# Layer 1's query product in two row tiles of 64 into two banks, with the product of keys and values packed

## The chip, the core and the metric

The kernel runs on one core of a Trainium2 chip. The core has five engines that work side by side and meet at semaphores: TensorE (matmuls, PE in the profile; PEld is its loading of weights), VectorE (DVE), ScalarE (ACT), GpSimd (POOL) and SyncE (SP), which issues the DMA transfers here. TensorE writes only to PSUM, eight banks of 128 partitions x 512 floats; VectorE and ScalarE read them. TensorE's clock has two levels, 1.2 and 2.4 GHz. The metric is the device time of one execution in microseconds.

## The reference, cut to what matters

Two conditioned attention layers over x of 32 sequences x 128 tokens x 512. Layer 0 is ordinary attention with 16 heads. Layer 1 is linear attention with 8 heads of 64, and the change is in it:

```python
xn = _ln(x, ln_w, ln_b)
q = xn @ Wq + bq
k = xn @ Wk + bk + (1.0 - src_mask) * -1000000.0
q = jax.nn.softmax(q.reshape(b, t, h, dh), axis=-1)   # h = 8, dh = 64
k = jax.nn.softmax(k.reshape(b, t, h, dh), axis=1)
v = ((xn @ Wv + bv) * src_mask).reshape(b, t, h, dh)
att = jnp.einsum('bnhd,bnhl->bhdl', k, v)
y = jnp.einsum('bnhd,bhdl->bnhl', q, att).reshape(b, t, d)
...
hh = _ln(y, ln2_w, ln2_b) * (1.0 + scale) + shift
hh = jax.nn.silu(hh) @ W_out + b_out
return x + hh
```

`att` is one 64 x 64 matrix for each head, and `y` multiplies each token's 64 query features of a head with it.

## The kernel before, in words

The sequences are worked in pairs (GROUP = 2), 16 pairs for each layer. One step of the program holds the attention and output of a pair k, the projections (keys, values, queries) of the next pair f, and the norm of the pair n after it. Steps 16 to 31 work layer 1's pairs (`step1` on each engine); most of them run in a loop whose body holds two steps. The order on each engine is written out by hand in `step1`, and engines meet at counting semaphores; nothing schedules it anew. Projections are exact-split float products: a matmul is written as three passes (lines 1276 to 1278).

The path around the change, for sequence b (0 or 1) of pair k:
- ScalarE's `k_exps` (line 644) takes the exponentials of a pair's keys, behind VectorE's maxima (`k_soft`, line 966).
- TensorE turns keys and queries (`turn_k` line 1387, `turn_q` line 1395) and ScalarE copies them out of PSUM (`kt_out` line 656, `qt_out` line 661). Both sequences' turned queries go to bank 3, one behind the other. In ScalarE's step the order is: copies of keys 0, queries 0 and keys 1; `k_out` and `k_exps` of pair f, first half; the copy of queries 1; `k_out` and `k_exps`, second half.
- `keys_values` (line 1407): for each of the four chunks c of 128 features, two matmuls of 64 x 64, one for each head, in two column tiles. They land on the diagonal blocks of a 128 x 128 square in bank 4.
- `kv_out` (line 1008) scales them on VectorE with two instructions, one for each diagonal half, into `kv_blocks`, whose off-diagonal blocks GpSimd has set to zero once, in the last step of layer 0 (the wait for `zeroed` is VectorE's).
- `query` (line 1417): for each chunk one matmul of 128 x 128 with the block-diagonal square, so two heads at once, into bank 5 (b = 0) or 1 (b = 1).
- `y_norm` (line 932) multiplies by the reciprocal of the softmax's sum, then come statistics (line 880), GpSimd's norm (lines 454 to 462), TensorE's turn (`turn_yn`, line 1368), the film scale (line 941), GpSimd's addition of the shift (line 488), tanh (line 632), silu (line 948), and the output product and its addition to x (line 960). SyncE stores x (line 331) and then loads the next x (line 316).

`claim(bank, ...)` makes TensorE wait for whoever last had to read the bank before it writes there again.

TensorE's step reads: turn k0, q0, k1; output of the last pair's second sequence; keys 0; turn q1; `keys_values` 0; keys 1; `query` 0; `keys_values` 1; values 0; `query` 1; queries 0; turn y0; values 1; turn y1; queries 1; turn x0; output 0; turn x1.

Of the kernel before, what the change touches and what calls it, by code (L numbers as in the profile page):

```python
# [8 lines left out]
ALU = mybir.AluOpType  # L9
# [3 lines left out]
P = 128  # L13
GROUP = 2
# [27 lines left out]
def done(stage, at):  # L42

    if at.reg is None and at.const < stage.first:
        return stage.always
    return stage.sem, (at + (1 - stage.first)).value()
# [9 lines left out]
def build(nc, t, out):  # L56
    B, T, D = t["x"].shape
    TE = t["cond_2048"].shape[1]
    C = D // P
    KE = TE // P  # L60
    N = GROUP * P
    G = B // GROUP
# [13 lines left out]
    H0, H1 = layers[0]["H"], layers[1]["H"]  # L76
# [7 lines left out]
    with ExitStack() as ctx:  # L84
# [3 lines left out]
        def sem(name):  # L88
            return ctx.enter_context(nc.semaphore(name))

        def chunks(ap):
            return ap.rearrange("p (c n) -> p c n", c=C)
# [76 lines left out]

        bank = [ctx.enter_context(nc.psum_tensor(f"bank{i}", [P, D], F32)) for i in range(8)]  # L170
        FIRST = dict(X=(0, 1), PT=(4, 5), Q=(6, 7), K=(0, 1), V=(3, 4), PV=(7, 7), Y=(2, 2), H=(6, 7), O=(5, 6))
        SECOND = dict(X=(0, 1), K=(6, 7), V=(0, 6), Q=(2, 4), KT=(2, 4), QT=(3, 3), KV=(4, 4), Y=(5, 1), H=(3, 7), O=(5, 7))

        MIXED = FIRST | dict(K=(6, 7), V=(0, 1), Q=(3, 4))

# [4 lines left out]
        per_seq = prob[:].rearrange("p a h n -> p (a h n)").rearrange("p (j d) -> p j d", d=D)  # L180
        k_tok = [per_seq[:, b, :] for b in range(GROUP)]
        q_feat = [per_seq[:, GROUP + b, :] for b in range(GROUP)]
        kv_blocks = [per_seq[:, 2 * GROUP + b, :] for b in range(GROUP)]
        k_max = sb("k_max", [P, 2, 2 * GROUP])
        k_sum = sb("k_sum", [P, 2, 2, 2 * GROUP])
        k_rec = sb("k_rec", [P, 2, 2, 2 * GROUP])
# [23 lines left out]
        w_in = [[sem(f"w_in{l}{j}") for j in range(4)] for l in range(2)]  # L210
        w_high = [[sem(f"w_high{l}{j}") for j in range(4)] for l in range(2)]
        w_split = [[sem(f"w_split{l}{j}") for j in range(4)] for l in range(2)]
        zeroed = sem("zeroed")
        wide_clear = sem("wide_clear")

        def stages(names, first=0):
# [218 lines left out]
        def _(pool):  # L435
# [70 lines left out]
            def step0(i, n, f, k, late, slot):  # L506
                norm1(n, 0)
                if i == 0:
                    pool.wait_ge(par_in[0], PARS[0])
                residual(0, k, 0)  # L510
                norm1(n, 1)
                norm2(k, 0)
                residual(0, k, 1)
                v_mask(f, slot, 0)
                if i == 0:
                    pool.wait_ge(film_dve, 3)
                add_shift(0, k, 0)
                norm2(k, 1)
                v_mask(f, slot, 1)
                if i == G - 1:  # L520

                    for g in range(2):
                        pool.wait_ge(*done(s[f"pt_pe{g}"], LAST0))
                    pool.memset(per_seq[:, 2 * GROUP:3 * GROUP, :], 0.0).then_inc(zeroed, 1)
                add_shift(0, k, 1)

            def step1(i, n, f, k, late, slot):
# [277 lines left out]
        def _(dve):  # L805
# [35 lines left out]
            def bias_col(l, j, i, b):  # L841
                dve.wait_ge(par_in[l], PARS[l])
                dve.wait_ge(bias_sum_pe, TURN[l, j])
                dve.tensor_tensor(col[:, l, i, :], col[:, l, i, :], bank[b][:, 0:C], ALU.add).then_inc(bias_dve, 1)
# [76 lines left out]
            def y_norm(l, k, kslot, b):  # L921
                dve.wait_ge(*done(s["y_pe"], k + b))
                dve.wait_ge(*done(s["stats2"], k + (b - 1)))
                dve.wait_ge(*done(s["yn_full"], k + (b - 1)))
                if l == 0:
                    dve.wait_ge(*done(s["rec"], k + b))
                    yb, h, rc = bank[FIRST["Y"][b]], H0, rec0[:, b, :]
                else:
                    dve.wait_ge(*done(s["qrec"], k + b))
                    yb, h, rc = bank[SECOND["Y"][b]], H1, q_rec[:, kslot, b, :]  # L930
                hv = lambda ap: ap.rearrange("p (h e) -> p h e", h=h)
                dve.tensor_tensor(hv(y_s[:]), hv(yb[:]),
                                  rc.rearrange("p (h o) -> p h o", o=1).broadcast_to([P, h, D // h]),
                                  ALU.mult).then_inc(s["y_norm"].sem, 1)
                dve.wait_ge(*done(s["y_norm"], k + b))
                moments(1, b, y_s[:], "stats2", "aggr2", k + b)

# [63 lines left out]
            def kv_out(k, kslot, b):  # L1001
                dve.wait_ge(*done(s["pv"], k + b))
                dve.wait_ge(*done(s["y_pe"], k + (b - GROUP)))
                dve.wait_ge(*done(s["krec"], k))
                for h in range(2):
                    q2 = slice(DH1 * h, DH1 * (h + 1))
                    rc = k_rec[q2, kslot].rearrange("p a (j g) -> p (a j) g", g=GROUP)[:, :, b:b + 1]
                    last = dve.tensor_tensor(chunks(kv_blocks[b])[q2, :, q2], chunks(bank[SECOND["KV"][b]][:])[q2, :, q2],
                                             rc.broadcast_to([DH1, C, DH1]), ALU.mult)
                last.then_inc(s["att_out"].sem, 1)  # L1010

            def start():
                f = pair(0)
# [32 lines left out]
            def step0(i, n, f, k, late, slot):  # L1046
                if late:
                    film_scale(0, late + (-1), 1)
                if i == G - 3:
                    spread_norm_b(1)  # L1050
                softmax(k, 0, (0, 1))
                if i == 0:
                    film(0, 5)
                if late:
                    silu(late + (-1), 1)
                softmax(k, 0, (2,))
                if late:
                    s_low_part(late + (-1), 1)
                softmax(k, 0, (3,))
                stats1(n, 0)  # L1060
                softmax(k, 1, (0, 1, 2))
                if late:
                    output(FIRST, late + (-1), 1)
                if i == 0:
                    embed_sum(1, 0, 6)
                softmax(k, 1, (3,))
                stats1(n, 1)
                sums_inverse(k, 0)
                y_norm(0, k, 1 - slot, 0)
                sums_inverse(k, 1)  # L1070
                v_add(0, FIRST, f, slot, 0)
                if i == 0:
                    embed_sum(1, 1, 6)
                if i == G - 3:
                    bias_col(1, WK, KB, 6)
                    dve.wait_ge(mask_saved, 16)
                    dve.wait_ge(film_dve, 3)
                film_scale(0, k, 0)
                if i == G - 2:
                    low_part(1, WK, (0, 1))  # L1080
                silu(k, 0)
                if i == G - 2:
                    bias_wide(1, WV, VALUE_BIAS[1], 3)
                y_norm(0, k, 1 - slot, 1)
                s_low_part(k, 0)
                xt_low(n, 1 - slot, 0)
                xt_low(n, 1 - slot, 1)
                v_add(0, FIRST, f, slot, 1)
                if i == G - 2:
                    low_part(1, WK, (2, 3))  # L1090
                    low_part(1, WV)
                output(FIRST, k, 0)
                if i == 0:
                    film(1, 6)
# [37 lines left out]
            def step1(i, n, f, k, late, slot):  # L1132
                if i == G:
                    film_scale(0, late + (-1), 1)
                    q_sums(k, 1 - slot, 0)
                    silu(late + (-1), 1)
                    q_sums(k, 1 - slot, 1)
                    s_low_part(late + (-1), 1)
                    dve.wait_ge(zeroed, 1)
                elif late:  # L1140
                    output(SECOND, late + (-1), 1)
                if n:
# [60 lines left out]
        def _(pe):  # L1203
# [194 lines left out]
            def keys_values(k, kslot, b):  # L1398
                to = SECOND["KV"][b]
                claim(to, (s["att_out"], k + b))  # L1400
                pe.wait_ge(*done(s["kt_out"], k + b))
                pe.wait_ge(*done(s["v_mask"], k + b))
                for c in range(C):
                    for h in range(2):
                        rows = slice(DH1 * h, DH1 * (h + 1))
                        head = slice(c * P + DH1 * h, c * P + DH1 * (h + 1))
                        last = pe.matmul(bank[to][rows, head], k_tok[b][:, head], v_s[:, kslot, b, head],  # L1407
                                         start=True, stop=True, tile_position=(0, DH1 * h))
                last.then_inc(s["pv"].sem, 1)

            def query(k, b):
                to = SECOND["Y"][b]
                claim(to, (s["y_norm"], k + b))
                pe.wait_ge(*done(s["att_out"], k + b))
                pe.wait_ge(*done(s["qt_out"], k + b))
                for c in range(C):
                    last = pe.matmul(bank[to][:, c * P:(c + 1) * P], q_feat[b][:, c * P:(c + 1) * P],  # L1417
                                     kv_blocks[b][:, c * P:(c + 1) * P], start=True, stop=True)
                last.then_inc(s["y_pe"].sem, 1)

            def start():
# [178 lines left out]
```

## Time and profile before

| | us |
|---|---|
| median of 3 runs (1095.82 to 1096.64) | 1095.91 |
| the profiled execution | 1097.78 |
| its span | 1096.0 |
| TensorE busy | 1054.8 (96%) |
| VectorE busy | 759.8 (69%) |
| ScalarE busy | 591.6 (54%) |
| GpSimd busy | 448.6 (41%) |

The span is what the trace covers; the execution's time has 1.78 us beside it. Busy times are sums over instructions. A float matmul is recorded as two passes, so the 128 matmuls of the query product stand in the trace as 256. Passes overlap: a pass lasts longer than the distance from its start to the next one's, and it is this distance that counts in a stream. "Idle before" is the time in which an engine had nothing to do ahead of an instruction, with the one that ended it.

### The profile page before, as it was taken

What the parts mean: (1) busy time and instruction counts of PE and PEld (TensorE: products, weight loads), DVE (VectorE), ACT (ScalarE), POOL (GpSimd) and SP (SyncE); (2) the same over time, 40 slices, a digit from 0 to 9 for tenths busy, and PEclk for the clock granted to TensorE, in tenths of its full rate; (3) what the DMA queues carried; (4) which work ended last, traced back from release to release, by engine and by line L of the source; (5) the groups of instructions that cost most, each with busy time, mean ns of one, the idle gap of its engine ahead of it and who ended that gap; (6) DMA issues with size and microseconds to landing.
All of it is one profiled execution on the core that took longest, in us unless ns stands there. A gap on an engine that the chain in (4) does not pass through costs nothing. (4 is left out here: it accounts for less than half of the span.)

```text
span 1096.0 us, 25953 instructions
## 1 busy us (share of the span) xinstructions
PE 1054.8 (96%) x8696; PEld 909.8 (83%) x8696; DVE 759.8 (69%) x1326; ACT 591.6 (54%) x1960; POOL 448.6 (41%) x783
## 2 busy tenths in 40 slices
PE   6999999999999999999999999999999999999995
PEld 4878888888888888888887778888888888888884
DVE  4656766676666766667678787777777777777764
ACT  5366667776677766776588443433343443434431
POOL 3242434334343343433343344444444444444432
PEclk9999999999999999999999999999999999999997
DMA  8824110111101111011102211111111111111011
GB/s 275 256 84 141 42 61 24 62 62 41 60 24 62 62 41 59 25 62 63 43 23 98 95 50 33 40 55 57 57 57 57 57 57 57 52 52 39 31 38 58
DMA packets 46017, 71.65 MB, mean 65 GB/s; under 512 B 10256, under 2 KB 14448, under 8 KB 45968
## 3 DMA queue, kind: packets, MB, share of 16 engines
q1 hardware_dynamic: 45968, 71.02, 20.3%
q8 instruction: 27, 0.44, 0.2%
q14 instruction: 22, 0.18, 0.1%
HBM read 54.19 MB, written 16.79 MB: 65 GB/s over the span
## 5 line engine op out<-in xcount | busy, mean ns | idle before, releaser
L1276 PE MATMUL bank<-xt_hi,w_hi 128*128 128x256 f32 x768 | 228.4, 297 | 3.1 <-DVE xt_lo L893 3.1
L1277 PE MATMUL bank<-xt_lo,w_hi 128*128 128x256 f32 x768 | 218.5, 284 | 0.0
L1278 PE MATMUL bank<-xt_hi,w_lo 128*128 128x256 f32 x768 | 218.3, 284 | 0.0
L454 POOL TENSOR_SCALAR stat<-stat 128x1 f32<-128x1 f32 x128 | 34.5, 270 | 441.8 <-DVE stat L884 417.7
L613 ACT ACTIVATE prob<-prob,neg_max 128x128 f32<-128x128 f32 x512 | 198.7, 396 | 6.7 <-DVE neg_max L907 6.6
L632 ACT ACTIVATE th<-z_s 128x512 f32<-128x512 f32 x64 | 40.5, 633 | 249.9 <-POOL z_s L488 249.8
L1276 PE MATMUL bank<-w_hi,xt_hi 128*128 128x512 f32 x384 | 158.3, 412 | 1.0 <-DVE w_lo L835 1.0
L1276 PEld LDWEIGHTS bank<-xt_hi,w_hi 128*128 128x128 f32 x768 | 148.9, 194 | 9.1 <-DVE w_lo L835 4.8
L1278 PE MATMUL bank<-w_hi,xt_lo 128*128 128x512 f32 x384 | 150.5, 392 | 0.0
L1277 PE MATMUL bank<-w_lo,xt_hi 128*128 128x512 f32 x384 | 149.8, 390 | 0.0
L1277 PEld LDWEIGHTS bank<-xt_lo,w_hi 128*128 128x128 f32 x768 | 148.6, 193 | 0.0
L1278 PEld LDWEIGHTS bank<-xt_hi,w_lo 128*128 128x128 f32 x768 | 148.2, 193 | 0.0
L1276 PE MATMUL bank<-w_hi,s_hi 128*128 128x512 f32 x256 | 106.7, 417 | 7.2 <-DVE s_lo L954 5.1
L488 POOL TENSOR_TENSOR z_s<-z_a,film_ab 128x512 f32<-128x512 f32 x64 | 68.5, 1071 | 107.2 <-DVE z_a L941 103.3
L1278 PE MATMUL bank<-w_hi,s_lo 128*128 128x512 f32 x256 | 101.1, 395 | 0.0
L1277 PE MATMUL bank<-w_lo,s_hi 128*128 128x512 f32 x256 | 100.5, 393 | 0.0
L613 ACT ACTIVATION_READ_ACCUMULATOR prob<-prob,neg_max 128x1 f32 x512 | 99.7, 195 | 0.0
L904 DVE TENSOR_TENSOR prob<-bank,mask_row 128x512 f32<-128x512 f32 x128 | 87.6, 684 | 12.7 <-PE bank L1327 12.1
L493 POOL TENSOR_TENSOR x_res<-x_res,bias_wide 128x512 f32<-128x512 f32 x64 | 88.7, 1386 | 16.2 <-DMA x_res<-between_layers 16.2
L621 ACT ACTIVATE room<-bank 128x512 f32<-128x512 f32 x128 | 74.4, 593 | 31.5 <-PE bank L1338 29.6
L907 DVE TENSOR_REDUCE neg_max<-prob 128x4 f32<-128x512 f32 x128 | 87.9, 687 | 4.4
L948 DVE SCALAR_TENSOR_TENSOR th<-th,z_s 128x512 f32<-128x512 f32 x64 | 47.2, 737 | 62.4 <-ACT th L632 61.4
(130 smaller groups left out, 2203.3 us busy)
## 6 DMA issues: line engine op xcount, KB each, us to landing
x_in<-in_x_dram SPq DMA_DIRECT2D x32, 256.0 KB, 2.8
x_res<-in_x_dram SPq DMA_DIRECT2D x32, 256.0 KB, 2.9
between_layers<-x_res SPq DMA_DIRECT2D x32, 256.0 KB, 2.0
x_in<-between_layers SPq DMA_DIRECT2D x32, 256.0 KB, 2.8
x_res<-between_layers SPq DMA_DIRECT2D x32, 256.0 KB, 2.8
out_dram<-x_res SPq DMA_DIRECT2D x32, 256.0 KB, 2.6
room<-in_L_cond_W_emb_dram SPq DMA_DIRECT2D x8, 512.0 KB, 7.3
prob<-in_L_cond_emb_w_dram SPq DMA_DIRECT2D x4, 512.0 KB, 7.5
```

Of the source, the lines that this page charges most:

```text
L454: pool.tensor_scalar(v[:, 8:9], v[:, 7:8], EPS, None, ALU.add).then_inc(s[a_in].sem, 1)
L488: pool.tensor_tensor(chunks(z_s[:, b, :]), chunks(z_a[:]), film_of(l, 1, k + b), ALU.add).then_inc(s["z_full"].sem, 1)
L493: pool.tensor_tensor(x_res[:, b, :], x_res[:, b, :], wide[:, OUT_BIAS[l], :], ALU.add).then_inc(s["res_full"].sem, 1)
L613: last = act.activation(prob[:, b, i, :], prob[:, b, i, :], ACT.Exp, bias=neg_max[:, b, i:i + 1], accum_out=row_sum[:, b, h:h + 1])
L621: act.activation(prob_t[:, g, :], bank[FIRST["PT"][g % 2]][:], ACT.Copy).then_inc(s[f"pt_out{g}"].sem, 1)
L632: act.activation(th[:], z_s[:, b, :], ACT.Tanh, scale=0.5).then_inc(s["tanh_full"].sem, 1)
L904: dve.tensor_tensor(prob[:, b, heads, :], bank[c][:].rearrange("p (r n) -> p r n", r=HC0), row, ALU.add).then_inc(s[f"masked{c}"].sem, 1)
L907: dve.tensor_reduce(neg_max[:, b, heads], prob[:, b, heads, :], AX.X, ALU.max, negate=True).then_inc(s[f"neg{c}"].sem, 1)
L948: dve.scalar_tensor_tensor(out=s_s[:], in0=th[:], scalar=1.0, in1=z_s[:, b, :], op0=ALU.add, op1=ALU.mult).then_inc(s["s_full"].sem, 1)
L1276: pe.matmul(o, a_hi, b_hi, start=start, stop=False)
L1277: pe.matmul(o, a_hi, b_lo, start=False, stop=False)
L1278: return pe.matmul(o, a_lo, b_hi, start=False, stop=stop)
```

## The change

`keys_values` writes its 64 x 64 blocks packed, 64 columns a chunk, so bank 4 holds 256 columns and no zero blocks. `kv_out` scales them with one instruction of 128 x 256. `query` makes two matmuls a chunk, one for each head: 64 rows of the turned queries (64 x 128, the weights) with a 64 x 64 block, in two row tiles, head 0's into the first bank and head 1's into the second. The first sequence's banks are 5 and 3, the second's 1 and 7. `y_norm` of layer 1 reads the two banks with two instructions of 128 x 256 and writes each head to its place. GpSimd's memset of the zero blocks and its semaphore go; VectorE waits in its place for the turned probabilities of layer 0, whose room the blocks take. Two waits of VectorE (`mask_saved`, `film_dve`) move from step 13 to step 0.

```diff
-        SECOND = dict(..., KV=(4, 4), Y=(5, 1), H=(3, 7), O=(5, 7))
+        SECOND = dict(..., KV=(4, 4), Y=((5, 3), (1, 7)), H=(3, 7), O=(5, 7))
...
-        kv_blocks = [per_seq[:, 2 * GROUP + b, :] for b in range(GROUP)]
+        kv_blocks = [per_seq[:, 2 * GROUP + b, 0:C * DH1].rearrange("p (c e) -> p c e", c=C) for b in range(GROUP)]
...
-                    for g in range(2):
-                        pool.wait_ge(*done(s[f"pt_pe{g}"], LAST0))
-                    pool.memset(per_seq[:, 2 * GROUP:3 * GROUP, :], 0.0).then_inc(zeroed, 1)
...
# y_norm, layer 1
-                hv = lambda ap: ap.rearrange("p (h e) -> p h e", h=h)
-                dve.tensor_tensor(hv(y_s[:]), hv(yb[:]),
-                                  rc.rearrange("p (h o) -> p h o", o=1).broadcast_to([P, h, D // h]),
-                                  ALU.mult).then_inc(s["y_norm"].sem, 1)
+                    for g in range(2):
+                        rc = q_rec[:, kslot, b, :].rearrange("p (c g) -> p c g", g=2)[:, :, g:g + 1]
+                        last = dve.tensor_tensor(y_s[:].rearrange("p (c g e) -> p g c e", c=C, g=2)[:, g],
+                                                 bank[SECOND["Y"][b][g]][:, 0:C * DH1].rearrange("p (c e) -> p c e", c=C),
+                                                 rc.broadcast_to([P, C, DH1]), ALU.mult)
+                last.then_inc(s["y_norm"].sem, 1)
...
# kv_out
-                for h in range(2):
-                    q2 = slice(DH1 * h, DH1 * (h + 1))
-                    rc = k_rec[q2, kslot].rearrange("p a (j g) -> p (a j) g", g=GROUP)[:, :, b:b + 1]
-                    last = dve.tensor_tensor(chunks(kv_blocks[b])[q2, :, q2], chunks(bank[SECOND["KV"][b]][:])[q2, :, q2],
-                                             rc.broadcast_to([DH1, C, DH1]), ALU.mult)
-                last.then_inc(s["att_out"].sem, 1)
+                rc = k_rec[:, kslot].rearrange("p a (j g) -> p (a j) g", g=GROUP)[:, :, b:b + 1]
+                dve.tensor_tensor(kv_blocks[b], bank[SECOND["KV"][b]][:, 0:C * DH1].rearrange("p (c e) -> p c e", c=C),
+                                  rc.broadcast_to([P, C, DH1]), ALU.mult).then_inc(s["att_out"].sem, 1)
...
# keys_values
-                        last = pe.matmul(bank[to][rows, head], k_tok[b][:, head], v_s[:, kslot, b, head],
+                        last = pe.matmul(bank[to][rows, c * DH1:(c + 1) * DH1], k_tok[b][:, head], v_s[:, kslot, b, head],
...
# query
-                claim(to, (s["y_norm"], k + b))
+                for h in range(2):
+                    claim(to[h], (s["y_norm"], k + b))
                 pe.wait_ge(*done(s["att_out"], k + b))
-                pe.wait_ge(*done(s["qt_out"], k + b))
+                if b == 1:
+                    pe.wait_ge(*done(s["qt_out"], k + b))
                 for c in range(C):
-                    last = pe.matmul(bank[to][:, c * P:(c + 1) * P], q_feat[b][:, c * P:(c + 1) * P],
-                                     kv_blocks[b][:, c * P:(c + 1) * P], start=True, stop=True)
+                    for h in range(2):
+                        rows = slice(DH1 * h, DH1 * (h + 1))
+                        last = pe.matmul(bank[to[h]][:, c * DH1:(c + 1) * DH1], q_feat[b][rows, c * P:(c + 1) * P],
+                                         kv_blocks[b][rows, c, :], start=True, stop=True, tile_position=(DH1 * h, 0))
```

The order of the instructions changes only where these stand. On TensorE, around the two query products of a step (`prob` is the room of the turned queries and the blocks; `w_hi`, `xt_hi` are the value projection between them), the rows before:

```order
L1417 MATMUL bank<-prob 128x128 [waits qt_out,att_out,o_out]
L1417 MATMUL bank<-prob 128x128 x3
L1407 MATMUL bank<-v_s,prob 64x64 [waits v_mask,kt_out,att_out]
L1407 MATMUL bank<-v_s,prob 64x64 x7
L1276 MATMUL bank<-w_hi,xt_hi 128x512 [waits xt_low]
...
L1417 MATMUL bank<-prob 128x128 [waits qt_out,att_out,xt_low]
L1417 MATMUL bank<-prob 128x128 x3
```

and after:

```order
L1421 MATMUL bank<-prob 128x64 [waits att_out,qt_out,o_out]
L1421 MATMUL bank<-prob 128x64 x7
L1406 MATMUL bank<-v_s,prob 64x64 [waits v_mask,kt_out,att_out]
L1406 MATMUL bank<-v_s,prob 64x64 x7
L1275 MATMUL bank<-w_hi,xt_hi 128x512 [waits xt_low]
...
L1421 MATMUL bank<-prob 128x64 [waits att_out,qt_out,kb_out,xt_low]
L1421 MATMUL bank<-prob 128x64 x7
```

Four matmuls became eight of half the columns, and the second query also waits for `kb_out`, the copy of keys from bank 7. The first one's `qt_out` has the same name but another count: it comes from the claim on bank 3 and is met by the copy of the second sequence's turned queries (k + 1), not of the first's (k).

On VectorE, from the scaled product of keys and values to the next step's statistics, before:

```order
L1008 TENSOR_TENSOR prob<-bank,k_rec 64x4x64 [waits krec]
L1008 TENSOR_TENSOR prob<-bank,k_rec 64x4x64
L966 TENSOR_REDUCE k_max<-q_t 128x4 [waits kexp0,ka_out]
L932 TENSOR_TENSOR y_s<-bank,q_rec 128x512 [waits yn_full,qrec,stats2,y_pe]
L880 BN_STATS stat<-y_s 128x6 [waits y_norm]
```

and after:

```order
L1005 TENSOR_TENSOR prob<-bank,k_rec 128x256 [waits krec]
L965 TENSOR_REDUCE k_max<-q_t 128x4 [waits kexp0,ka_out]
L930 TENSOR_TENSOR y_s<-bank,q_rec 128x4x64 [waits yn_full,qrec,stats2,y_pe]
L930 TENSOR_TENSOR y_s<-bank,q_rec 128x4x64
L874 BN_STATS stat<-y_s 128x6 [waits y_norm]
```

One instruction fewer stands ahead of the maxima, and one more at the normalising of y.

## Rows read from the trace of the kernel before

**Rows 1.** The page, busy time of the engines over the span.

```profile
PE 1054.8 (96%) x8696; PEld 909.8 (83%) x8696; DVE 759.8 (69%) x1326; ACT 591.6 (54%) x1960; POOL 448.6 (41%) x783
```

**Rows 2.** Busy time of each engine in one step of layer 1.

```profile
core 0: us, PE busy (x) PEld busy (x) DVE busy (x) ACT busy (x) POOL busy (x), PEclk, DMA share, GB/s
898.70:928.60 29.90, 29.81 (x207) 25.71 (x205) 22.31 (x39) 10.86 (x31) 13.45 (x24) 1.00 0.18 57
```

**Rows 3.** TensorE in order of time around both query products (start, length, instruction).

```profile
897.87 1.06 PE L1417 MATMUL bank<-prob 128*128 128x128 f32 x8
898.86 0.69 PE L1407 MATMUL bank<-v_s,prob 128*64 128x64 f32 x16
...
899.81 0.39 PE L1277 MATMUL bank<-w_lo,xt_hi 128*128 128x512 f32 x1
...
902.10 0.39 PE L1278 MATMUL bank<-w_hi,xt_lo 128*128 128x512 f32 x1
902.33 1.05 PE L1417 MATMUL bank<-prob 128*128 128x128 f32 x8
...
903.45 0.40 PE L1277 MATMUL bank<-w_lo,xt_hi 128*128 128x512 f32 x1
```

**Rows 4.** The film product, line 1264: durations in ns, first and last start.

```profile
L1264 PE MATMUL bank<-pick,spare x16: 195/276/276, 83.8 to 85.4; 128*128 128x32 f32 x16
```

**Rows 5.** TensorE in order of time around layer 0's scores, line 1327.

```profile
302.23 1.04 PE L1338 MATMUL bank<-ident,prob 128*128 128x128 f32 x8
303.20 1.17 PE L1327 MATMUL bank<-room,q_t 32*128 32x128 f32 x32
304.30 0.50 PE L1276 MATMUL bank<-w_hi,s_hi 128*128 128x512 f32 x1
304.64 0.39 PE L1277 MATMUL bank<-w_lo,s_hi 128*128 128x512 f32 x1
```

**Rows 6.** By line and shape, 560 to 1090 us: busy, mean ns, idle before.

```profile
L1407 PE MATMUL bank<-v_s,prob 128*64 128x64 f32 x512 | 21.9, 228 | 0.7 <-ACT prob L656 0.7
...
L1008 DVE TENSOR_TENSOR prob<-bank,k_rec 64x256 f32<-64x256 f32 x64 | 27.0, 422 | 2.8 <-PE bank L1407 1.6
...
L932 DVE TENSOR_TENSOR y_s<-bank,q_rec 128x512 f32<-128x512 f32 x32 | 22.0, 687 | 35.8 <-PE bank L1417 35.8
```

**Rows 7.** TensorE, the first query of the first, eleventh and fifteenth step.

```profile
627.11 1.06 PE L1417 MATMUL bank<-prob 128*128 128x128 f32 x8
...
927.75 1.06 PE L1417 MATMUL bank<-prob 128*128 128x128 f32 x8
...
1047.32 1.06 PE L1417 MATMUL bank<-prob 128*128 128x128 f32 x8
```

**Rows 8.** ScalarE, the copy of the second turned queries in four steps.

```profile
627.08 0.57 ACT L661 ACTIVATE prob<-bank 128x512 f32<-128x512 f32 x1
...
898.12 0.57 ACT L661 ACTIVATE prob<-bank 128x512 f32<-128x512 f32 x1
...
928.65 0.57 ACT L661 ACTIVATE prob<-bank 128x512 f32<-128x512 f32 x1
...
1047.50 0.57 ACT L661 ACTIVATE prob<-bank 128x512 f32<-128x512 f32 x1
```

**Rows 9.** VectorE in order of time within that step.

```profile
898.97 0.69 DVE L932 TENSOR_TENSOR y_s<-bank,q_rec 128x512 f32<-128x512 f32 x1 [2.44 <-PE bank L1417]
...
906.71 0.69 DVE L941 TENSOR_TENSOR z_a<-bank,film_ab 128x512 f32<-128x512 f32 x1 [1.20 <-PE bank L1368]
...
908.75 1.32 DVE L988 TENSOR_TENSOR room<-spare,q_max 128x512 f32<-128x512 f32 x1
910.22 0.69 DVE L948 SCALAR_TENSOR_TENSOR th<-th,z_s 128x512 f32<-128x512 f32 x1 [0.15 <-ACT th L632]
...
924.25 0.69 DVE L880 BATCH_NORM_STATS2 stat<-x_in 128x6 f32<-128x512 f32 x1 [0.82 <-DMA x_in<-between_layers]
```

**Rows 10.** GpSimd's additions (line 488): one behind the memset, one in that step.

```profile
616.87 1.05 POOL L488 TENSOR_TENSOR z_s<-z_a,film_ab 128x512 f32<-128x512 f32 x1 [5.39 <-DVE z_a L941]
...
908.47 1.05 POOL L488 TENSOR_TENSOR z_s<-z_a,film_ab 128x512 f32<-128x512 f32 x1
```

More of the change, by code:

```diff
@@ L171, in build @@
         FIRST = dict(X=(0, 1), PT=(4, 5), Q=(6, 7), K=(0, 1), V=(3, 4), PV=(7, 7), Y=(2, 2), H=(6, 7), O=(5, 6))
-        SECOND = dict(X=(0, 1), K=(6, 7), V=(0, 6), Q=(2, 4), KT=(2, 4), QT=(3, 3), KV=(4, 4), Y=(5, 1), H=(3, 7), O=(5, 7))
+        SECOND = dict(X=(0, 1), K=(6, 7), V=(0, 6), Q=(2, 4), KT=(2, 4), QT=(3, 3), KV=(4, 4), Y=((5, 3), (1, 7)), H=(3, 7), O=(5, 7))
         MIXED = FIRST | dict(K=(6, 7), V=(0, 1), Q=(3, 4))
@@ L212, in build @@
         w_split = [[sem(f"w_split{l}{j}") for j in range(4)] for l in range(2)]
-        zeroed = sem("zeroed")
         wide_clear = sem("wide_clear")
@@ L519, in step0 @@
                 v_mask(f, slot, 1)
-                if i == G - 1:
-                    for g in range(2):
-                        pool.wait_ge(*done(s[f"pt_pe{g}"], LAST0))
-                    pool.memset(per_seq[:, 2 * GROUP:3 * GROUP, :], 0.0).then_inc(zeroed, 1)
                 add_shift(0, k, 1)
@@ L926, in y_norm @@
                     dve.wait_ge(*done(s["rec"], k + b))
-                    yb, h, rc = bank[FIRST["Y"][b]], H0, rec0[:, b, :]
+                    last = dve.tensor_tensor(y_s[:].rearrange("p (h e) -> p h e", h=H0),
+                                             bank[FIRST["Y"][b]][:].rearrange("p (h e) -> p h e", h=H0),
+                                             rec0[:, b, :].rearrange("p (h o) -> p h o", o=1).broadcast_to([P, H0, DH0]),
+                                             ALU.mult)
                 else:
                     dve.wait_ge(*done(s["qrec"], k + b))
-                    yb, h, rc = bank[SECOND["Y"][b]], H1, q_rec[:, kslot, b, :]
-                hv = lambda ap: ap.rearrange("p (h e) -> p h e", h=h)
-                dve.tensor_tensor(hv(y_s[:]), hv(yb[:]),
-                                  rc.rearrange("p (h o) -> p h o", o=1).broadcast_to([P, h, D // h]),
-                                  ALU.mult).then_inc(s["y_norm"].sem, 1)
+                    for g in range(2):
[4 more added lines that the diff above has]
+                last.then_inc(s["y_norm"].sem, 1)
                 dve.wait_ge(*done(s["y_norm"], k + b))
@@ L1075, in step0 @@
                     bias_col(1, WK, KB, 6)
+                if i == 0:
                     dve.wait_ge(mask_saved, 16)
@@ L1138, in step1 @@
                     s_low_part(late + (-1), 1)
-                    dve.wait_ge(zeroed, 1)
+                    for g in range(2):
+                        dve.wait_ge(*done(s[f"pt_pe{g}"], LAST0))
                 elif late:
```

## The prediction, made before the changed kernel ran

> **What bounds the kernel now.** I read the page first: TensorE is busy for 96% of the span, VectorE for 69% [rows 1]. Then the stretches: in one step of the second layer's loop TensorE is busy for 29.81 of 29.90 us at full clock, every other engine for at most 22.31 [rows 2]. So TensorE's stream is the path there, and what is added to it or makes it wait is paid in each of the 16 steps. The table by line says who waits: VectorE, 35.8 us in all, for the query product (line 1417) [rows 6]. Last I read the order in time of TensorE, ScalarE and VectorE around that product, to see what stands ready and what only just.
>
> **TensorE's own work.** A query product is 4 matmuls, recorded as 8 passes. It starts at 902.33 and the second matmul behind it at 903.45. Of these 1.12 us, 0.23 belong to the first matmul behind it (the spacing of such matmuls, 902.10 to 902.33), which leaves 0.89 us, 0.11 a pass, and nothing for changing over [rows 3]. After the change there are 8 matmuls, 16 passes, in 8 pairs of two row tiles. Each pass streams 64 columns in place of 128, but still loads 128 columns of weights. Three rows bear on the spacing of a pair:
> - The film product (line 1264) loads 128 columns of weights and streams only 32; its 16 passes start from 83.8 to 85.4, so 1.6 / 15 = 0.107 us apart [rows 4]. With a quarter of the stream the spacing is that of the full one: the load sets it.
> - Layer 0's scores (line 1327) are four row tiles with 128 columns loaded and 128 streamed. 32 passes take 1.17 us, the last of them about 0.27, so (1.17 - 0.27) / 8 = 0.11 a group of four [rows 5]. Row tiles do run side by side, loads too, and a group is no faster than one pass.
> - The product of keys and values (line 1407) has 64 columns on both sides, in two column tiles. 16 passes take 0.69 us, one of them 0.23: 0.03 each, 0.06 a pair [rows 3, 6].
> The bounds of a pair are 0.06 and 0.11 us. I take 0.11, as the film product is the row with many columns to load and few to stream. The 8 pairs then take 0.89 us as before, and the halved stream gives nothing. The other end is worth 8 x 0.05, about 0.42 us a query.
> The Trainium skill says, in "TensorE: Matmul & The Clock Gate", section "LDWEIGHTS (loading the stationary operand)", that a weight load's time follows its columns and not its rows. By this rule the eight loads of 128 columns stay and the sum would be mine; the film product's trace agrees, though with full rows only. "TensorEngine Tiling (Array Packing)" of the Trainium skill, section "Theoretical Speedup", gives up to 2x for a small dimension of 64; by it the sum would be that of the first rival below.
>
> **Changing over.** The scores also show what going into and out of row tiles costs. From the turned probabilities in front (8 passes, 0.88) at 302.23 they start at 303.20: 0.09 lost. Then it is 1.10 us to the next product, for 8 x 0.11: 0.22 lost, of which I put half behind the first group. The first matmul behind takes 0.34 instead of 0.23: 0.11. Sum 0.42 us [rows 5]. The product of keys and values pays for its own: 0.11 in front (0.99 for 8 x 0.11) and some 0.26 within and behind (0.95 less 0.23 and 8 x 0.06) [rows 3]. The second query of a step stands between untiled products, so it now pays 0.42. The first is followed directly by the product of keys and values, whose change is paid already; it adds the way in, 0.09 + 0.11 = 0.20. Straight from row tiles to column tiles stands in no row; I leave it at what is paid there now, bounds 0 (a change saved, -0.11) and 0.2 more. **Per step +0.62 us**, over 16 steps 9.9.
>
> **The new wait.** The first query now writes banks 5 and 3, and bank 3 holds the second sequence's turned queries until ScalarE has copied them (line 661). Before, it asked for the first copy alone. The second stands in ScalarE's queue behind four exponentials of the next pair (line 644), which wait for VectorE's maxima. The query starts at 897.87 and that copy runs from 898.12 for 0.57, so it ends 0.82 later; one step on it is 927.75 against 929.22, 1.47 later. In the first step it is 0.54, in the fifteenth 0.75 [rows 3, 7, 8]. I took all fifteen starts and ends: of the 14 behind the first step seven are late by 1.34 to 1.67 (mean 1.51) and seven by 0.75 to 1.01 (mean 0.88). The last step has no such exponentials and no wait. Behind the stopped query stand all of TensorE's products of the step.
> What moves that copy: the scaling of keys times values on VectorE (line 1008) goes from two instructions of 0.42 us to one with as many columns, 0.42 less ahead of the maxima [rows 6]. One engine wakes another in about 0.04: VectorE starts at 898.97 on a product that ends at 897.87 + 1.06 [rows 3, 9]. Net, the copy is 0.38 us earlier.
> Does the wait come back in each step? The way to the copy is a circle: query (897.87), VectorE's normalising of y (898.97), y turned on TensorE, film scale (906.71), line 988, silu (910.22), output, the store and load of x, its statistics (924.25, held by the DMA), then line 1008, maxima, exponentials and the copy [rows 3, 8, 9]. A later query makes a later next copy, so each step pays anew. TensorE's own 0.62 delays the film scale, for y is turned behind both queries. But line 988 takes 1.32 us there, with as many columns as the 0.69 of line 932; GpSimd's addition at 908.47 ends at 909.52 and line 988 0.55 behind it [rows 9, 10]. A start 0.6 later meets a free GpSimd and ends at about the same time. So I count 0 here and keep 0.45 (0.6 less the slack of 0.15 ahead of 910.22) as the other bound. The normalising of y becomes two instructions, 2 x 0.42 for 0.69, +0.15, and the second line 1008 on the same way gives back 0.42; both lie ahead of the gap of 1.20 at 906.71 [rows 6, 9]. If that gap were gone, they would give 0.27 more.
> A step thus grows by the larger of 0.62 (TensorE's work) and its lateness less 0.38: 1.13 in the late steps, and 0.50, so 0.62, in the others.
>
> **The sum.** 7 x 1.13 + 7 x 0.62 = 12.2. The first step's wait is 0.54 + 0.04 = 0.6 (there another product holds the maxima, and VectorE's saving does not count). TensorE's work behind the query of step fifteen: 0.6. The last step is latency from end to end: the ways in and +0.15 of VectorE for each sequence, less 0.42 ahead of each query, about 0.2 in all. Together 13.6 us. GpSimd's memset, once, goes too; it stood ahead of an addition that waits 5.39 us for VectorE [rows 10], so nothing for it, and if that wait were gone, at most its own length of about one addition. The profiled execution took 1097.78 us, 1.78 beside its span; with the sum 1111.4. It lies 1.87 above the median of the runs, so **1109.5 us** there, +1.24%.
>
> **Rivals.**
> - A pair takes 0.06 us. TensorE's step is 0.62 - 2 x 0.42 = -0.22 us, and the end of the query comes 0.42 earlier, so lateness less 0.80: 0.71 in the late steps, 0.08 in the others. 7 x 0.71 + 7 x 0.08 = 5.5, 0.6 in the first step, -0.3 at the end: +6, 1102. For it: the column-tiled rows at 0.06 have the same stream. Against: they load half the columns. 0.20.
> - The later turn of y is not absorbed at line 988: lateness + 0.07 in each step, 14 x (1.19 + 0.07) = 17.6, and 1.4 at the ends: 1115. Against it stands the row of 1.32 us; for it, that such a lock can be met anew elsewhere. 0.18.
> - Not slower: the copy's way is no circle, and the wait is paid once, 1.5 us. From there TensorE's work decides alone. With a pair at 0.06 this is 1.5 - 16 x 0.22 = -2.0, so 1093.9; the sign turns at a pair of about 0.11 - 0.62 / 16 = 0.07 us, below which each step gains. With 0.11 it gives +11, 1107. For it: VectorE is busy 22 of 30 us and could run ahead. Against: the links above. 0.07, and 0.03 for a draw beside it.
> - The row tiles don't run side by side, so the change doesn't do what it says: 8 x 0.11 more a query, 32 times, +38 with the rest: 1134. Against: the scores. 0.03.
> The forecast itself has 0.49.
>
> **The numbers.** The range reaches below the first rival and above the second, 2 us each for the small terms: 1100 to 1117. Outside are the third and the last rival and the tails. What a measurement of this kernel can tell from no change is about 0.2%. Faster by more than that has 0.07, within it 0.03, slower 0.90.
>
> **What would show it.** In the profile after, the query's line has 16 passes with pairs 0.11 apart (or 0.06). The first query of a step is held by ScalarE's copy of the turned queries, in every other step by about 0.5 us. Steps take 30.5 and 31.0 us in place of 29.9. The first matmul behind a second query takes 0.34 to its next. TensorE's idle time in the second layer is some 4 us more. The prediction is wrong if the wait does not show, if the pairs stand nearer 0.06, or if the straight change from row to column tiles costs several tenths more.

## The result, and the profile after

The changed kernel took 1107.22 us (median of 6, 1105.84 to 1109.77) beside 1096.73 of the kernel before: ratio 1.0097, 95% interval 1.0081 to 1.0112. That is +10.5 us, where 13.6 were forecast (1109.5 from a median of 1095.91). The profiled execution is the slowest of the six, 1109.77.

The page of the changed kernel, its span and busy times:

```profile
span 1108.0 us, 26479 instructions
...
PE 1062.6 (96%) x8952; PEld 912.8 (82%) x8952; DVE 739.1 (67%) x1326; ACT 593.6 (54%) x1960; POOL 446.8 (40%) x782
```

VectorE has 21 us less work and TensorE 8 more [rows 1]. TensorE of the changed kernel in order of time, around both queries of the tenth step (line 1421 is the query, 1406 keys times values, 1275 to 1277 the projections):

```profile
906.53 0.28 PE L1277 MATMUL bank<-xt_hi,w_lo 128*128 128x256 f32 x1
906.95 1.11 PE L1421 MATMUL bank<-prob 64*128 64x64 f32 x16
907.98 0.69 PE L1406 MATMUL bank<-v_s,prob 128*64 128x64 f32 x16
...
911.23 0.39 PE L1277 MATMUL bank<-w_hi,xt_lo 128*128 128x512 f32 x1
911.55 1.11 PE L1421 MATMUL bank<-prob 64*128 64x64 f32 x16
912.59 0.50 PE L1275 MATMUL bank<-w_hi,xt_hi 128*128 128x512 f32 x1
912.93 0.39 PE L1276 MATMUL bank<-w_lo,xt_hi 128*128 128x512 f32 x1
```

and ScalarE of the same kernel, the copy of the second sequence's turned queries (line 655):

```profile
906.27 0.57 ACT L655 ACTIVATE prob<-bank 128x512 f32<-128x512 f32 x1
```

The copy ends at 906.84 and the query starts at 906.95. It is so in all fifteen steps that could wait: each first query starts 0.09 to 0.11 us behind the end of that copy. Before, it started 0.54 to 1.67 ahead of it [rows 7, 8]. The second query shows the price of row tiles: 911.23 to 911.55 is 0.32 where 0.23 is usual, 1.04 to the next product, 0.34 to the one after. From 911.23 to 912.93 it is 1.70 us, against 1.35 from 902.10 to 903.45 [rows 3]: **+0.35**. The first takes 1.03 to the next product instead of 0.99, and what follows it takes as long as before.

The steps, as the distance from one first query to the next: 29.89 us before (mean of the 13 from 658.73 to 1047.32), 30.47 after (663.07 to 1059.21). After the change they alternate, 30.26 to 30.34 and 30.59 to 30.80; 30.5 and 31.0 were forecast. The page's 12.0 us more are thus: 13 x 0.58 = 7.5 in these steps, 2.6 in the step ahead of them (31.62 before, 34.20 after), 0.1 behind the last, and 1.8 up to the first query, of which 1.1 is there already at layer 0's first scores (44.83 and 45.92). That 1.1 is scatter between executions: in the bank 2 kernel below, which is the same program up to there, the scores start at 44.19. So the mechanism stands in nearly every step, and a fifth of the loss in one.

### The profile page after: what moved, and what is told of

Read it like the earlier page. It is cut to its first block and busy times, and to the rows that moved or that the text cites. A ratio compares the mean times of both kernels' runs of the same rounds, so it can differ in the third digit from the quotient of the medians.

```text
span 1108.0 us, 26479 instructions
## 1 busy us (share of the span) xinstructions
PE 1062.6 (96%) x8952; PEld 912.8 (82%) x8952; DVE 739.1 (67%) x1326; ACT 593.6 (54%) x1960; POOL 446.8 (40%) x782
## 5 line engine op out<-in xcount | busy, mean ns | idle before, releaser
L638 ACT ACTIVATE q_t<-q_t,k_max 128x128 f32<-128x128 f32 x128 | 49.8, 390 | 74.3 <-DVE k_max L965 74.3
```

Of the source, the lines that this page charges most:

```text
L638: last = act.activation(v[:, i, :], v[:, i, :], ACT.Exp, bias=k_max[:, pair, i:i + 1], accum_out=k_sum[:, slot, pair, i:i + 1])
```

## The experiments

All steps below are means of the same 13 steps. Ratios are against the kernel before on the same chip.

### The wait taken out: the second tile of the first query in bank 2

```diff
-        Y=((5, 3), (1, 7))
+        Y=((5, 2), (1, 7))
...
-                if b == 1:
-                    pe.wait_ge(*done(s["qt_out"], k + b))
+                pe.wait_ge(*done(s["qt_out"], k + b))
```

> The changed kernel with one number other: the first query's second tile goes to bank 2 (free between the copy of keys 0 and the next queries) in place of bank 3, and asks for its own copy of turned queries only. Theory (the wait on bank 3 and TensorE's work share the loss; a stall of TensorE on s_lo that was there before goes too): no wait at the first query, steps of 29.9 + 0.49 - 0.2 to 0.4 = 30.0 to 30.2 us, the time 4 to 7 us under the changed kernel, so +3 to +6 on before. Rival (TensorE's added work alone makes the loss, the wait only takes the place of other idle time): under 1 us gained, +9 to +10.

Measured: 1101.77 us, ratio 1.0045 (1.0031 to 1.0058), so the choice of bank 3 costs about half of the loss. The theory's numbers came true (5.5 us gained, 4.5 left, steps of 30.05). Busy time of the engines over the 13 steps (window, then PE, PEld, DVE, ACT and POOL with their instructions, clock, DMA share, GB/s):

```profile
659.61:1050.21 390.60, 390.60 (x2861) 334.44 (x2860) 269.51 (x505) 150.30 (x417) 177.50 (x309) 1.00 0.16 51
```

By its busy time TensorE never stands still; each step is 30.04 or 30.05. In this kernel the copy still ends behind the query's start, but no instruction waits for it. TensorE of the bank 2 kernel in order of time, the queries of two neighbouring steps:

```profile
899.98 1.11 PE L1419 MATMUL bank<-prob 64*128 64x64 f32 x16
...
930.03 1.11 PE L1419 MATMUL bank<-prob 64*128 64x64 f32 x16
```

and its ScalarE, the copy of either step:

```profile
899.54 0.57 ACT L655 ACTIVATE prob<-bank 128x512 f32<-128x512 f32 x1
...
930.08 0.57 ACT L655 ACTIVATE prob<-bank 128x512 f32<-128x512 f32 x1
```

The copies end at 900.11 and 930.65, 0.13 and 0.62 behind the queries' starts, against 0.82 and 1.47 before. With 30.05 as the stream's own length, the wait in the changed kernel is 30.47 - 30.05 = 0.42 us a step: by the single steps 0.21 to 0.29 in one and 0.54 to 0.75 in the next.

### The wait alone

```diff
-                pe.wait_ge(*done(s["qt_out"], k + b))
+                pe.wait_ge(*done(s["qt_out"], k + 1))
```

> The kernel before, with nothing but the first query waiting for the copy of the second sequence's turned queries. Theory (a circle, paid in each step): steps grow by the lateness 1.19 + 0.10 of wake-up, less up to 0.4 of stalls that it replaces: 0.9 to 1.3 in 14 steps and 0.6 in the first, +13 to +19 us. Rival (paid once): +1.5 to +2 us.

Measured: 1118.64 us, ratio 1.0197 (1.0183 to 1.0211), +21 us, above even the upper end. TensorE's waits from 640 to 1060 us (in total, times, longest):

```profile
PE bank L1417 <- ACT prob L661: 16.5, 13, 1.9
PE bank L1276 <- DVE s_lo L954: 1.5, 5, 0.7
```

Steps are 31.38, +1.49. The circle is real and paid each time. The expectation took up to 0.4 off for standstills that the wait would replace. It replaced none: the one on s_lo (see below) is as long in this kernel as before, since it lies behind the query and not ahead of it. That gives 1.29; the last 0.2 a step is open. In the changed kernel the same wait costs only 0.42; the next experiment shows how much of that packing can account for.

### Packing undone, row tiles kept

As the bank 2 kernel, with the blocks back on the diagonal and two instructions to scale them:

```diff
-                        last = pe.matmul(bank[to][rows, c * DH1:(c + 1) * DH1], k_tok[b][:, head], ...
+                        last = pe.matmul(bank[to][rows, head], k_tok[b][:, head], ...
...
-                                         kv_blocks[b][rows, c, :], ...
+                                         kv_blocks[b][rows, c * P + DH1 * h:c * P + DH1 * (h + 1)], ...
```

> As x_bank2, row tiles into banks 5 and 2, but keys times values not packed: blocks on the diagonal as before, scaled by two instructions of VectorE. Against x_bank2 it gives the worth of packing alone. Theory: VectorE's 0.42 shorter way also removed TensorE's wait for s_lo (0.3 to 0.4 a step), so without packing it is 2 to 5 us slower than x_bank2. Rival (VectorE is no limit once the wait on bank 3 is gone): within 1 us of x_bank2.

Measured: 1101.62 us, ratio 1.0045 (1.0031 to 1.0059). The rival was right: without the wait on bank 3, packing is worth nothing that shows. Steps are 30.09 against 30.05. But the copy of the turned queries ends 0.66 to 0.90 and 1.46 to 1.97 us behind the query's start without packing (first step left out), and 0.11 to 0.22 and 0.48 to 0.72 with it. So packing brings the copy forward by 0.6 us and more, and that would keep the wait on bank 3 small; the changed kernel without packing was not run.

### What sets the spacing of a pair

Two edits of the bank 2 kernel, each of which leaves out a part of the output and was executed once (1101.92 and 1095.81 us).

```diff
-                        last = pe.matmul(bank[to[h]][:, c * DH1:(c + 1) * DH1], ...
-                                         kv_blocks[b][rows, c, :], ...
+                        last = pe.matmul(bank[to[h]][:, c * DH1:c * DH1 + 32], ...
+                                         kv_blocks[b][rows, c, 0:32], ...
```

> As x_bank2, but each row-tiled matmul streams only 32 of the 64 columns (the other half of each head's output is left out). Theory (the load of 128 columns of weights sets the spacing of a pair): pairs stay 0.105 us apart. Rival (the stream sets it): 0.05 to 0.06.

TensorE of this kernel in order of time, the query and the next product:

```profile
901.30 1.08 PE L1419 MATMUL bank<-prob 64*128 64x32 f32 x16
902.32 0.69 PE L1406 MATMUL bank<-v_s,prob 128*64 128x64 f32 x16
```

And with half of the weights' columns in three of four chunks:

```diff
+                        m = P if c == 0 else DH1
-                        last = pe.matmul(bank[to[h]][:, c * DH1:(c + 1) * DH1], q_feat[b][rows, c * P:(c + 1) * P],
+                        last = pe.matmul(bank[to[h]][0:m, c * DH1:(c + 1) * DH1], q_feat[b][rows, c * P:c * P + m],
```

> As x_bank2, but of the four chunks three load only 64 columns of weights (tokens 64 to 127 of their output are left out), with 64 columns streamed. Theory (load sets it): pairs of those chunks 0.058 us apart, the query 6 x 0.047 = 0.28 us shorter. Rival (stream or issue sets it): 0.105 as before.

TensorE of this kernel, the same two instructions:

```profile
897.38 0.93 PE L1420 MATMUL bank<-prob 64*128 64x64 f32 x16
898.24 0.69 PE L1406 MATMUL bank<-v_s,prob 128*64 128x64 f32 x16
```

The starts of single passes give the spacing. In the bank 2 kernel one pair starts 0.112 us behind the other (the 0.105 of the expectations is the distance from a pair's second pass to the next pair's first). With half the stream it stays 0.112, and the query takes 1.02 to the next product instead of 1.04. With half the load it is 0.058 once the halved chunks are under way, and the query takes 0.86. That is 0.18 less, not the expected 0.28, for around the first halved pair the distances are 0.21 and 0.11. The steps: 29.99 and 29.69 us. The load of 128 columns sets the pair, as the forecast had it from one row [rows 4], and the rival at 0.06 is refuted for this product. "TensorE: Matmul & The Clock Gate" of the Trainium skill, section "LDWEIGHTS (loading the stationary operand)", says that the time of a weight load goes by its columns, whatever its rows. Here the trace agrees in row tiles of 64 rows too: 0.112 us with 128 columns, 0.058 with 64.

### The row tiles in turn

```diff
-                for c in range(C):
-                    for h in range(2):
+                for h in range(2):
+                    for c in range(C):
```

> As x_bank2, but the query's eight matmuls stand in another order: the four chunks of head 0 in the upper row tile, then the four of head 1 in the lower, so neighbours share a row tile. Theory (two row tiles hide each other's loads, and the load of 128 columns sets the spacing): 14 of 16 passes 0.105 to 0.11 us apart instead of a pair in that time, the query some 0.75 us longer, steps of 31.4 to 31.6 us. Rival (the order does not matter, since the queue looks ahead over the loads): steps within 0.1 us of 30.05.

Executed once: 1116.31 us beside 1096.17, steps 31.05, the query 1.60 long instead of 1.11. It fits neither number. Passes in one tile stand 0.112 apart; only where head 0's last meet head 1's first do the two tiles run side by side, by themselves, for half of each head's passes. So alternating is worth 0.49 us a query, and a part of the overlap comes without it.

### Fewer changes of tiling: both products of keys and values side by side

On the kernel before; the second one moves ahead of the second half of the keys' projection.

```diff
-        KV=(4, 4)
+        KV=(4, 2)
...
                     keys_values(k, 1 - slot, 0)
+                    keys_values(k, 1 - slot, 1)
...
                     query(k, 0)
-                    keys_values(k, 1 - slot, 1)
```

> The kernel before with both products of keys and values of a step side by side (the second into bank 2), so TensorE changes into column tiles and back once a step and not twice; no row tiles, no packing. Theory (a change of tiling costs 0.35 to 0.37 us and TensorE's stream is the path): -0.35 a step in 15 steps, 3 to 6 us faster than before. Rival (VectorE's and ScalarE's circle is the limit at 29.9 as well, or the stream closes the gap elsewhere): within 1.5 us of before.

Measured: 1109.7 us, ratio 1.0113 (1.0098 to 1.0129): 12.4 us slower, by more than the change itself, steps 30.76. TensorE's waits from 650 to 1060 us:

```profile
PE bank L1276 <- DVE s_lo L954: 9.7, 26, 0.4
```

Neither number fits: the theory took TensorE's stream for the path, and the rival had another circle hold the step at 29.9, but saw no loss. No wait on a bank shows, only the one on s_lo. The reading is a second circle: first query, y and its norm, silu, s_lo; then TensorE's output product, keys, and the next first query. The moved product used to run behind the first query, while the other engines worked on y. Now it runs ahead of the query, so it makes the circle longer and TensorE has less to do while it waits. The kernel before shows the same wait, small: TensorE in order of time, four turned passes and what follows them, in the kernel before,

```profile
916.86 0.60 PE L1387 MATMUL bank<-ident,q_t 128*128 128x128 f32 x4
917.55 0.47 PE L1276 MATMUL bank<-w_hi,s_hi 128*128 128x512 f32 x1
```

and in the changed kernel:

```profile
896.09 0.60 PE L1386 MATMUL bank<-ident,q_t 128*128 128x128 f32 x4
896.44 0.47 PE L1275 MATMUL bank<-w_hi,s_hi 128*128 128x512 f32 x1
```

0.69 against 0.35 us from start to start. In the kernel before it is 0.68 to 0.76 in nearly every step. With both products side by side it is 0.93 to 0.96, and the output of the first sequence waits too: 1.00 from the turned x ahead of it, where 0.35 is usual. Before, TensorE stood still for about 0.34 us in each step, and the "busy" of 29.81 in 29.90 [rows 2] hid it, for a pass is recorded longer than it holds the engine.

### A later addition on GpSimd

What makes s_lo late in the kernel before? VectorE in order of time in the kernel before; s_lo takes 0.99 where 0.69 is usual, and silu ahead of both, at 914.85, takes 0.87:

```profile
915.63 0.68 DVE L979 TENSOR_TENSOR spare<-bank,bias_wide 128x512 f32<-128x512 f32 x1
916.42 0.99 DVE L954 TENSOR_TENSOR s_lo<-th,s_hi 128x512 fp32r<-128x512 f32 x1
```

GpSimd adds the output's bias to x beside it (line 493, from 915.15 for 1.71). The experiment lets it do so later:

```diff
                 if k:
+                    if n:
+                        pool.wait_ge(*done(s["xt_low"], n + 1))
                     residual(1, k, 1)
```

> The kernel before; only GpSimd's addition of the output bias for the second sequence (line 493 there, 1.7 us beside VectorE's silu and s_lo) waits until VectorE has made xt_lo of the next pair, and so runs later. Theory (TensorE's 0.34 us a step of standing still on s_lo came from VectorE's two instructions being slowed by that addition, 0.87 and 0.99 us where 0.69 is usual): s_lo comes 0.4 to 0.5 earlier, steps of 29.6 to 29.7 us in place of 29.89, 3 to 5 us faster than before. Rival (the addition slows VectorE elsewhere as much, or another link of the circle holds): within 1.5 us of before.

Measured on the kernel before: **1093.64 us, ratio 0.9965 (0.9952 to 0.9979)**, faster than both kernels and by as much as the theory said. VectorE of this kernel in order of time; s_lo takes its usual 0.69:

```profile
912.69 0.86 DVE L950 SCALAR_TENSOR_TENSOR th<-th,z_s 128x512 f32<-128x512 f32 x1 [1.82 <-ACT th L634]
913.47 0.68 DVE L981 TENSOR_TENSOR spare<-bank,bias_wide 128x512 f32<-128x512 f32 x1
914.25 0.69 DVE L956 TENSOR_TENSOR s_lo<-th,s_hi 128x512 fp32r<-128x512 f32 x1
```

and over the 13 steps, of 29.58 us on the mean, TensorE is never idle by its busy time:

```profile
659.11:1043.65 384.54, 384.54 (x2655) 333.83 (x2654) 284.35 (x505) 149.25 (x417) 171.10 (x309) 1.00 0.17 52
```

By the starts it still stands still for 0.07 in every other step (0.43 where 0.36 is usual). The steps without that are 29.55, the length of the stream before, and 30.05 - 29.55 = **0.50 us a step is TensorE's added work**; 0.34 of it went into the time that it had stood still. One part of the expectation failed: silu stays at 0.86, so it is not this addition that slows it (another of GpSimd's, at line 482, lies beside its start; not tried).

The same on the changed kernel:

> The changed kernel with the same later addition. Theory (the wait on bank 3 is the end of a circle through VectorE's silu and s_lo): the circle is 0.4 to 0.5 shorter, the query's start is held for 0 to 0.2 us and steps shrink from 30.47 to 30.05 to 30.15, 4 to 6 us faster than the changed kernel. Rival (the copy's time is set by the landing of x or by ScalarE alone): within 1.5 us of the changed kernel.

Measured: 1106.76 us, ratio 1.009 (1.0077 to 1.0104). That is within a microsecond of the changed kernel (ratio 1.0097), with steps of 30.37: the theory's 4 to 6 us are refuted. VectorE there:

```profile
921.76 0.69 DVE L955 TENSOR_TENSOR s_lo<-th,s_hi 128x512 fp32r<-128x512 f32 x1
...
930.59 0.42 DVE L1007 TENSOR_TENSOR prob<-bank,k_rec 128x256 f32<-128x256 f32 x1 [0.23 <-PE bank L1408]
```

The 0.3 us are gained at s_lo, but now line 1007 waits for TensorE's own product of keys and values. That is a third, short way: that product, its scaling, the maxima, four exponentials, the copy, the query. From the product's start to the query's it takes 4.02 us in every other step, and 3.81 in the bank 2 kernel, where nothing waits for the copy. So it is longer by 0.2 than the keys' projection that TensorE does meanwhile, whatever comes ahead; hence the least wait of 0.2 in every other step of the changed kernel. In the other steps the way takes 4.27 with the later addition: line 1007 starts 0.90 behind the product's start instead of 0.73, and why is open. Another bank takes the wait away, as shown; another order on ScalarE was not tried.

## Why the prediction was right, and where it was off

**Right.** The direction, and that it is paid at two places in each step: TensorE's own work and the first query's wait on bank 3. The pair at 0.11 (0.112 measured), set by the load. The straight change from row to column tiles costs nothing beyond what was there (907.98 to the next product 0.62, as before). Line 988 did take up the later film scale: in the changed kernel it is

```profile
918.24 0.71 DVE L987 TENSOR_TENSOR room<-spare,q_max 128x512 f32<-128x512 f32 x1
919.09 0.69 DVE L947 SCALAR_TENSOR_TENSOR th<-th,z_s 128x512 f32<-128x512 f32 x1
```

0.71 instead of 1.32, and silu starts 12.1 us behind the query where it was 12.35 [rows 9]. VectorE's instructions cost as taken (groups by line and shape of the changed kernel, 560 to 1100 us: sum, mean ns, idle time ahead):

```profile
L930 DVE TENSOR_TENSOR y_s<-bank,q_rec 128x256 f32<-128x256 f32 x64 | 24.2, 420 | 60.6 <-PE bank L1421 58.0 <-POOL yn L461 2.6
...
L1005 DVE TENSOR_TENSOR prob<-bank,k_rec 128x256 f32<-128x256 f32 x32 | 13.6, 425 | 4.4 <-PE bank L1406 3.4
```

though the pair at the normalising takes 0.76 together, not 0.84 [rows 6].

**Mis-sized.** Three terms, all of the rule that a step grows by the larger of 0.62 and its lateness less 0.38:
- "Per step +0.62 us" measured 0.49 to 0.50: the second query adds 0.35, not 0.42, and the first 0.14 where it does not wait (bank 2 kernel), not 0.20.
- "TensorE's stream is the path there, and what is added to it is paid": in truth 0.34 us a step was a standstill on s_lo and took up that much, so only 0.16 of the added work was paid. The step that failed is the first view: I read a busy share and not the distances between starts.
- The wait beyond the stream: 0.26 a step was forecast (7 x 0.51 in 14), 0.42 measured. The floor of 0.2 from the short way was not seen. Two of its parts were off as well: from the scaling's start to the maxima it is 0.55 less (0.34 for 0.89), not 0.42, and the wake-up behind the copy is 0.10, not 0.04.

Together 0.58 a step (0.16 + 0.42) against 0.87 forecast, 7.5 us against 11.3 in 13 steps. Behind the fifteenth first query 0.8 was forecast and about 0.1 measured.

**Luck.** The total is nearer than its parts. Of the page's 12.0 us 1.1 is scatter, which leaves 10.9. Of these, 2.0 come from one step (2.6 less the 0.58 of a usual one) for a reason that the forecast did not have. Without it the change would have cost 8.9 us where 13.6 were forecast.

**Not foreseen.** The step with the output weights' split, between the first query of steps 16 and 17. TensorE of the changed kernel, busy time (PE, clock, DMA share, GB/s):

```profile
640.00:646.00 6.00, 4.36 (x24) 1.00 0.00 0
646.00:650.00 4.00, 3.42 (x9) 0.57 0.00 0
650.00:654.00 4.00, 4.00 (x27) 1.00 0.00 0
```

and what it does there:

```profile
643.76 0.60 PE L1271 MATMUL bank<-ident,xn 128*128 128x128 f32 x4
646.58 0.77 PE L1275 MATMUL bank<-w_hi,s_hi 128*128 128x512 f32 x1 [2.23 <-DVE s_lo L953]
```

It waits for s_lo for 2.23 us, where it was 0.77 before, and then the granted clock is at its lower level, 1.2 GHz, for most of four microseconds (0.57 on the mean, 0.50 from 647 to 649).

The s_lo is made 1.28 us later behind the first query (17.57 instead of 16.29). 0.40 of it is the later turn of y, which is not taken up in this step; the forecast had counted it as nothing, with 0.45 as the other bound. The other 0.89 is VectorE's split of the weights, which lies ahead of s_lo. VectorE and GpSimd (norm of the second y, addition of the shift) there, before:

```profile
636.45 2.90 DVE L835 SCALAR_TENSOR_TENSOR w_lo<-room,w_hi 128x512 fp32r<-128x512 f32 x4
636.97 1.85 POOL L462 TENSOR_SCALAR yn<-y_s,stat 128x512 f32<-128x512 f32 x1 [0.21 <-POOL stat L457]
638.79 1.48 POOL L488 TENSOR_TENSOR z_s<-z_a,film_ab 128x512 f32<-128x512 f32 x1
```

and after:

```profile
638.61 3.79 DVE L829 SCALAR_TENSOR_TENSOR w_lo<-room,w_hi 128x512 fp32r<-128x512 f32 x4
638.53 1.28 POOL L461 TENSOR_SCALAR yn<-y_s,stat 128x512 f32<-128x512 f32 x1 [0.21 <-POOL stat L456]
639.77 1.47 POOL L487 TENSOR_TENSOR z_s<-z_a,film_ab 128x512 f32<-128x512 f32 x1
```

The two engines race. Where the norm starts behind the split (0.52 us before), the addition comes so late that only the last of the four instructions of the split is long, 1.10. Where it starts ahead (0.08 in the changed kernel), the addition lies beside two of them, 1.09 and 1.53. The traces of all eleven kernels agree with this. The norm starts 0.05 to 0.09 ahead in the changed one, with bank 2, with half the stream and in the changed one with the later addition: split 3.76 to 3.79, wait 2.16 to 2.23. With the row tiles in turn it is 0.60 ahead, the split takes 3.37 and the wait 1.80. It starts 0.10 to 0.52 behind in the kernel before, there with the wait alone or the later addition, with packing undone and with half the load: split 2.90, wait 0.74 to 0.77. With both products side by side it is 1.92 behind, and no such wait shows. So less than 0.2 us between two starts decides about 0.9 us, and packing is one of the things that tip it (0.23 behind without, 0.06 ahead with it, both in bank 2); no run moved this order alone.

The clock is a second matter. It fell in two of the four profiled executions with the wait of 2.2 (the changed kernel and half the stream, steps of 34.20 and 34.01) and not in the two others (32.87 and 32.94), so it costs 1.1 to 1.3 us where it falls. That the changed kernel's six times fall into 1105.8 to 1106.4 and 1108.0 to 1109.8 would fit a clock that falls in some executions; only one of them was profiled, so this is not shown.

## What to carry to other kernels

A loop whose main engine is "busy" for 99.7% can still be bound by a circle: measure the distances between the starts of equal passes, and ask of each instruction that is moved or added whether it lies inside the circle or beside it. A small product in row tiles gains nothing where its weights keep their 128 columns, and pays about 0.35 us for changing the tiling; what shortened it was to halve the side that is loaded (0.18 us a query with three of four chunks halved). And a bank picked for a new tile brings its reader's whole queue into the wait: the same change costs 5.5 us less with the neighbouring bank.

## What the runs showed of the hardware that was not expected

- Into row tiles and out again costs 0.35 us (0.09 ahead, 0.05 behind the first pair, 0.21 in the two products behind, with 8 pairs of 0.11).
- Row tiles in turn still overlap at the seam of the two (1.60 us, not 16 x 0.11): the first four passes of the second tile run beside the last four of the first.
- A difference of less than 0.2 us in which of VectorE and GpSimd starts first made four VectorE instructions take 3.79 us in all or 2.90.
- The wake-up from ScalarE's copy to TensorE is 0.10 to 0.11 us in front of a row-tiled product and 0.15 in front of the full one; from TensorE to VectorE it was 0.04 [rows 3, 9].
